# Both attentions: a wide score row's second-half maximum starts from the first half's, and the combining pass on VectorE is dropped

## The chip, the cores and the metric

The kernel runs on one core of a Trainium2 chip. The metric is the device time of one execution in microseconds (us), the median of several runs.

## The reference: two transformer layers with causal attention

The input x is (4, 1024, 128). Four steps follow each other, each added to x behind a layer norm. Only the two attentions matter here; both are causal and have 16 heads.

```python
# first attention (a0 in the kernel), head width 8
scores = jnp.einsum('bhqd,bhkd->bhqk', q, k) * scale
scores = jnp.where(causal, -inf, scores)
attn = jax.nn.softmax(scores, axis=-1)
out = jnp.einsum('bhqk,bhkd->bhqd', attn, v)
...
# second attention (a1), 16 heads over a shared latent of 32 for keys and values
attn = jax.nn.softmax(jnp.where(mask, attn, neg_inf), axis=-1)
```

After each attention comes a mixture of experts (8 experts, two of them chosen, then 16 experts, eight chosen), which the change leaves alone.

## The kernel before: scores are computed twice, once for the maximum of a row and once for the exponential

One function, `attention`, is called for both: as a0 with HG = 4 heads at a time (16 groups) and as a1 with HG = 2 (32 groups). Three kinds of work run interleaved.

**The maxima (S).** For each head the 1024 query rows are cut into eight blocks i = 0 to 7 of 128 rows. Block i sees (i+1)*128 keys. TensorE multiplies queries by keys into one of four PSUM banks `S` of 512 columns (L777). Blocks 4 to 7 are wider than a bank, so they are two units, half 0 with 512 keys and half 1 with the other 128 to 512. I call them 7a and 7b, 6a and 6b and so on, and 3a, 2a, 1a, 0a the narrow ones: 12 units a head, four of them second halves. The order in a head is `BLOCKS`: 7a 7b 3a 6a 6b 2a 5a 5b 1a 4a 4b 0a. For each unit VectorE does three things in a row: a one-column `memset` that carries the wait for TensorE's `unit_ready` (L676), a fused add of the causal mask and maximum over the row (L679, CUSTOM_DVE_ANT_0 in the profile), and the read of its accumulator into `mhalf` ("mh") for half 0 of a wide block or into `mmax` ("m") for all others (the second row of L679, DVE_READ_ACCUMULATOR2_ANT). Behind the last unit of a head, 0a, comes the combining pass: it waits for the last read, and takes the maximum of `mmax` and `mhalf` for the four wide blocks (L686, 128x4). Then TensorE transposes the head's maxima (unit "m", L782), ScalarE copies them negated (L717), and a DMA puts them as one more row into the queries of the next use (`set_row`). Each step that ends on VectorE raises `red_done`; TensorE waits for it before a bank is written again, which is four units later (units m and o count as well).

**The exponentials (T).** For each head nine pieces of 512 columns of transposed scores (L838) go into one of two banks `T`, ScalarE takes the exponential (L736), GpSimd zeroes the triangle on the diagonal (L647). One piece of one head is a slot: 36 slots in a group of a0, 18 in one of a1. TensorE waits before slot n for the exponential of slot n-2.

**The values (V).** Behind every HG-th slot TensorE multiplies a piece's probabilities by the values (L817). ScalarE copies the sums out (L712), TensorE turns them (unit "o", L788), VectorE divides them: a reciprocal (L692), a wait for it, a multiplication (L694).

TensorE's order is written out: slot by slot T, then the S, m or o units that belong to this slot, then V where one is due. The S units of slots are those of a later group: they work one or two groups ahead. In a group of a0 the last head's maxima are turned (m3) in slot 32, directly behind 0a in slot 31 and a V. Slot 33 has 7a 7b, slot 34 has 3a, slot 35 has 6a 6b 2a and a V, and slots 0 to 3 of the next group 5a 5b, 1a, 4a 4b, 0a with a V behind it. Before the first group of each attention stands a start stretch in which only maxima are made: all heads of group 0 and six units of group 1, on a ring of six banks.

Of the kernel before, what the change touches and what calls it, by code (L numbers as in the profile page):

```python
# [10 lines left out]
ALU = mybir.AluOpType  # L11
# [5 lines left out]
BATCH, SEQ = 4, 1024  # L17
TOK = BATCH * SEQ
TILES = TOK // P
ST = 512  # L20
# [430 lines left out]
def attention(k, name, HG, VD, scale, operands, out, work, begin, before_loads, lent=(),  # L451
              PARTS=1, BURST=1, HALVES=2):
    nc, sem = k.nc, k.sem
    NG = BATCH * HEADS // HG
# [9 lines left out]
    LEAD = 4  # L464
    BLOCKS = [b for i in reversed(range(TPB // 2)) for b in (TPB // 2 + i, i)]
    PBUF = 3 * BURST if BURST == 1 else 2 * BURST
    assert NP % BURST == 0 and 2 * NP % PBUF == 0
# [9 lines left out]
    for h in range(HG):  # L477
        blocks = [("S", h, i) for i in BLOCKS]
        chain += blocks[:2] + ([("m", h - 1, 0)] if h else []) + blocks[2:]
    chain.append(("m", HG - 1, 0))  # L480

    def units_from(items):

        return [(kind, h, i, half, ahead, min(n, NSLOT - 1)) for n, (kind, h, i, ahead) in enumerate(items)
                for half in range(HALVES if kind == "o" or kind == "S" and i >= TPB // 2 else 1)]

# [3 lines left out]
    for kind, h, i, half, _, _ in units_from([(*x, 0) for x in chain]):  # L491
        if kind == "S":
            NRED += 3 if i == BLOCKS[-1] and HALVES == 2 else 2
            MAXIMA[h, i, half] = NRED
    lead, own = [(*x, 0) for x in chain[:LEAD]], [(*x, 1) for x in chain[LEAD:]]
    start_units = units_from([(*x, 0) for x in chain] + [(*x, 1) for x in chain[:LEAD]])
    NLEAD = len(units_from(lead))
    NU = len(start_units) - NLEAD
# [3 lines left out]
    assert 2 * (NU + HALVES) % BANKS == 0  # L502
    base_items = own + [(*x, 2) for x in chain[:LEAD]]

    DELAY = HG
    VALUES, CARRIED = ({s: [] for s in range(NSLOT)} for _ in range(2))
    for p in range(NP):
        for part in range(PARTS):  # L510
            s = (p // BURST * BURST + BURST) * HG - 1 + DELAY + part * (HG // PARTS)
            (VALUES[s] if s < NSLOT else CARRIED[s - NSLOT]).append((p, part))
    parts = {}
    for p, piece in enumerate(PIECES):
        off = 0
        for seg in piece:
            for part in range(PARTS):
                c0, c1 = max(off, part * (ST // PARTS)), min(off + seg[2] - seg[1], (part + 1) * (ST // PARTS))
                if c0 < c1:
                    parts.setdefault((p, part), []).append((seg, c0, seg[1] + c0 - off, seg[1] + c1 - off))  # L520
# [3 lines left out]
    COPY_0 = next(s for s in VALUES if (LAST_OF_BANK[0], PARTS - 1) in VALUES[s]) + 1  # L524
    COPY_1 = max(s for s in CARRIED if CARRIED[s]) + 1
    OUT_AT = COPY_1 + 2
    out_item = ("o", 0, 0, -1)
    with_out = lambda items: units_from(items[:OUT_AT] + [out_item] + items[OUT_AT:])

    with ExitStack() as c:  # L530
# [41 lines left out]

        def units_of(g):

            if at(g, NG - 1):
                return [(*x[:5], OUT_AT) for x in units_from([out_item])]
            if at(g, NG - 2):
                return with_out(own)
            return units_from(base_items) if at(g, 0) else with_out(base_items)

        def before(g):

            if at(g, 0):
                last_of = {n % len(start_ring): x for n, x in enumerate(start_units)}
                return [last_of[bank] for bank in main_ring(unit_slot(g))]
            units = units_from(own if at(g, NG - 1) else base_items)
            return [(*x[:4], x[4] - 1, x[5]) for x in units[-BANKS:]]
# [27 lines left out]
        with nc.Block() as block:  # L615
# [37 lines left out]
            def _(dve):  # L653
                def consume(units, base, ring, g):
                    for n, (kind, h, i, half, ahead, _) in enumerate(units):
# [6 lines left out]
                        if kind == "S":  # L662
# [38 lines left out]
                consume(units_from([("o", 0, 0, 0)]), unit_base(END) + HALVES, main_ring(unit_slot(END) + HALVES), END)  # L701

            @block.scalar
            def _(act):
# [21 lines left out]
                def step(g):  # L726
                    units = units_of(g)
                    for p in range(NP):
                        for h in range(HG):
# [16 lines left out]
                            if slot == COPY_0:  # L746
                                copy_out(g, 0)
                            if slot == COPY_1 and not at(g, 0):
# [1674 lines left out]
```

## Time and profile before

| what | value |
|---|---|
| three runs, median (lowest to highest) | 2078.56 us (2075.58 to 2084.6) |
| the profiled execution's own time | 2072.83 us |
| its span | 2071.1 us |
| TensorE matmul busy | 1879.1 us, 91% |
| VectorE busy | 1435.9 us, 69% |
| ScalarE busy | 1193.8 us, 58% |
| GpSimd busy | 622.0 us, 30% |
| first and last start of a T matmul in a0 | 81.6 and 614.7 us |
| the same in a1 | 1038.0 and 1692.9 us |

The two attentions take more than half of the span. The busy time of TensorE counts overlapping matmuls, whose ends are modelled, so 91% is not 91% of its peak.

### The profile page before, as it was taken

The numbers are of one execution on the slowest core, as the hardware profiler recorded it, in microseconds if no ns is written. First come the engines' busy times: TensorE is split into PE (matmuls) and PEld (weight loads), VectorE is DVE, ScalarE is ACT, GpSimd is POOL, SyncE is SP. The second block draws the span as 40 slices with busy tenths as digits, with TensorE's granted clock in tenths as the row PEclk, the third lists the DMA queues.
The fourth block names the chain that finished last, engine by engine and source line by source line (L and its number), as shares of the span: only waits on it lengthen the run. The fifth ranks groups of instructions, "written<-read, shape, count | busy, mean of one in ns | idle before, by whom it ended". The sixth has DMA issues, their size and how long they took to land. (4 is left out here: it accounts for less than half of the span.)

```text
span 2071.1 us, 39995 instructions
## 1 busy us (share of the span) xinstructions
PE 1879.1 (91%) x9924; PEld 1169.6 (56%) x9926; DVE 1435.9 (69%) x6257; ACT 1193.8 (58%) x2252; POOL 622.0 (30%) x955
## 2 busy tenths in 40 slices
PE   5799999999986729994899999999999999899998
PEld 3455555555536527872445555555555558678886
DVE  6788777777826827875766666666666636887776
ACT  5266666666664728981445555555555558555554
POOL 4011111111120774762011111111111110567665
PEclk9799999999995869996989999999999999999999
DMA  6423233433305112224946464655555512546562
GB/s 214 123 35 64 42 61 44 61 48 55 49 8 207 36 56 70 75 76 132 362 112 145 104 139 106 136 111 130 116 126 122 119 35 81 138 93 131 128 121 61
DMA packets 107198, 210.87 MB, mean 102 GB/s; under 512 B 16540, under 2 KB 46378, under 8 KB 105680
## 3 DMA queue, kind: packets, MB, share of 16 engines
q1 hardware_dynamic: 99840, 194.98, 40.8%
q0 software_dynamic: 4992, 8.48, 1.3%
q10 hardware_dynamic: 2256, 6.21, 1.0%
q8 instruction: 37, 0.61, 0.1%
q14 instruction: 73, 0.60, 0.1%
HBM read 163.01 MB, written 47.89 MB: 102 GB/s over the span
## 5 line engine op out<-in xcount | busy, mean ns | idle before, releaser
L679 DVE CUSTOM_DVE_ANT_0 a1ms<-a1S,mask_q 128x128 bf16<-128x128 f32 (+1 forms) x758 | 387.9, 553 | 173.5 <-issue 170.6
L736 ACT ACTIVATE a1work<-a1T 128x512 f32<-128x512 f32 x576 | 330.2, 597 | 297.4 <-PE a1T L838 296.9
L679 DVE CUSTOM_DVE_ANT_0 a0ms<-a0S,mask_q 128x384 bf16<-128x384 f32 (+2 forms) x752 | 379.7, 553 | 97.5 <-issue 90.4
L736 ACT ACTIVATE a0work<-a0T 128x512 f32<-128x512 f32 x576 | 330.0, 597 | 186.6 <-PE a0T L838 175.7
L817 PE MATMUL a1O<-a1work,a1v 128*33 128x512 f32 (+3 forms) x1536 | 304.6, 496 | 0.9 <-POOL a1work L647 0.9
L838 PE MATMUL a0T<-a0qT,a0kT 128*128 128x512 f32 (+3 forms) x768 | 265.3, 392 | 15.9 <-ACT a0work L736 5.1
L838 PE MATMUL a1T<-a1qT,a1kT 97*128 97x512 f32 (+3 forms) x768 | 263.3, 391 | 2.0 <-DMA a1qT<-a1mr 2.0
L838 PEld LDWEIGHTS a1T<-a1qT,a1kT 97*128 97x128 f32 x768 | 131.6, 189 | 202.0 <-ACT a1work L736 144.5
L777 PE MATMUL a0S<-a0kS,a0qS 128*128 128x384 f32 (+2 forms) x752 | 229.9, 362 | 17.2 <-PEq L305 9.1
L1997 POOL TENSOR_TENSOR attn<-attn 128x512 f32<-128x512 f32 x136 | 201.4, 1496 | 105.8 <-DVE attn L1899 104.7
L838 PEld LDWEIGHTS a0T<-a0qT,a0kT 128*128 128x128 f32 x768 | 131.4, 189 | 170.2 <-ACT a0work L736 126.5
L777 PE MATMUL a1S<-a1kS,a1qS 96*128 96x128 f32 (+1 forms) x758 | 219.8, 351 | 2.5 <-DVE a1held L676 1.7
L643 POOL TENSOR_TENSOR a1held<-ident 128x1 f32<-128x1 f32 x160 | 30.9, 193 | 600.6 <-ACT a1work L736 600.6
L1886 DVE TENSOR_TENSOR r1late<-attn,r1late 128x512 fp32r<-128x512 f32 x136 | 120.4, 886 | 70.7 <-ACT r1late L2202 70.3
L643 POOL TENSOR_TENSOR a0held<-ident 128x1 f32<-128x1 f32 x80 | 15.5, 193 | 492.6 <-ACT a0work L736 492.6
L777 PEld LDWEIGHTS a0S<-a0kS,a0qS 128*128 128x128 f32 x752 | 139.7, 195 | 40.6 <-DVE a0held L676 19.2
L2202 ACT CAST r1late<-attn 128x512 fp32r<-128x512 f32 x136 | 84.5, 622 | 133.8 <-POOL attn L1997 127.9
L817 PE MATMUL a0O<-a0work,a0v 128*9 128x512 f32 (+3 forms) x1536 | 150.7, 487 | 0.0
L777 PEld LDWEIGHTS a1S<-a1kS,a1qS 96*128 96x128 f32 x758 | 138.7, 193 | 15.3 <-DVE a1held L676 4.1
L817 PEld LDWEIGHTS a1O<-a1work,a1v 128*33 128x33 f32 x1536 | 64.7, 109 | 108.7 <-issue 81.1
L1365 POOL DMA_INDIRECT scr_pairs<-stage x92 | 104.5, 1136 | 66.5 <-issue 33.4
L1090 DVE TENSOR_TENSOR m_hl<-m_h,m_hh 128x512 fp32r<-128x512 f32 x124 | 85.5, 690 | 32.6 <-ACT m_hh L1524 18.7
(336 smaller groups left out, 3333.2 us busy)
## 6 DMA issues: line engine op xcount, KB each, us to landing
attn<-scr_g SPq DMA_DIRECT2D x32, 1024.0 KB, 9.8
a1qT<-scr_q SPq DMA_DIRECT2D x93, 256.0 KB, 4.1
a1qS<-scr_q SPq DMA_DIRECT2D x90, 256.0 KB, 6.3
a1kT<-scr_k SPq DMA_DIRECT2D x93, 128.0 KB, 4.8
a1kS<-scr_k SPq DMA_DIRECT2D x90, 128.0 KB, 7.0
scr_q<-p_own SPq DMA_DIRECT2D x16, 512.0 KB, 5.1
scr_q<-attn SPq DMA_DIRECT2D x16, 512.0 KB, 7.4
scr_slots<-wp SPq DMA_DIRECT2D x1, 5980.0 KB, 18.2
```

Of the source, the lines that this page charges most:

```text
L643: nc.gpsimd.tensor_tensor(held[:, BANKS + p:BANKS + p + 1], k.ident[:, 0:1], k.ident[:, 0:1], ALU.add).then_inc(masked, 1)
L679: nc.vector.tensor_tensor_reduce(masked_s[spare][:, 0:c1 - c0], buf[:, 0:c1 - c0], k.mask_q[:, SEQ - w + c0:SEQ - w + c1], 1.0, NEVER, ALU ...
L736: nc.scalar.activation(prob_of(g, p)[:, h, :], t_ps[slot % 2][:, :], ACT.Exp, scale=scale)\
L777: last = nc.tensor.matmul(buf[:, c0 - first:c1 - first], qS[gU[1]][0:SROWS, h, i * P:(i + 1) * P], kS[gU[1]][0:SROWS, KI(h), c0:c1], start ...
L817: last = nc.tensor.matmul(o_ps[h * CT:h * CT + VW, q0:q1], vst[g[1]][:, seg[0], KI(h), :], prob_of(g, p)[:, h, off:off + q1 - q0], start=o ...
L838: last = nc.tensor.matmul(t_ps[slot % 2][:, off:off + q1 - q0], kT[g[1]][0:TROWS, KI(h), j * P:(j + 1) * P], qT[g[1]][0:TROWS, h, q0:q1], ...
L1090: tt(hl[n % HBUF][:, :], h[n % 2][:, :], hh[n % HBUF][:, :].bitcast(F32), ALU.subtract).then_inc(hl_ready, 1)
L1365: nc.gpsimd.indirect_dma_start(pair_rows, bass.IndirectOffsetOnAxis(ap=xt[t % XBUF][:, i, D + 1:ROW].bitcast(U32), axis=0), yo[t % XBUF][: ...
L1886: tt(hl[ring(g, e)][:, :], h[two(g, e)], hh[ring(g, e)][:, :].bitcast(F32), ALU.subtract).then_inc(hl_ready, 1)
L1997: nc.gpsimd.tensor_tensor(h[two(g, e)], prod[two(g, e)], gate, ALU.mult).then_inc(h_ready, 1)
L2202: nc.scalar.copy(hh[ring(g, e)][:, :], h[two(g, e)]).then_inc(hh_ready, 1)
```

## The change: the maximum of half 1 is seeded with that of half 0

The fused add-and-maximum takes a start value as its fourth argument from the end: so far the constant NEVER for all units. For half 1 it becomes a column in SBUF, the maximum that half 0 of the same block has left in `mhalf`. So that this column is there, VectorE waits for its own `red_done` ahead of each half 1. The combining pass and its wait go. The rest of the diff writes the options that both calls used (PARTS = 1, BURST = 1, HALVES = 2) into the function, and gives the slot of each unit as a table.

```diff
+class Order:
+    def __init__(self, blocks, mark, units, values, outs):
+        self.blocks, self.mark, self.units, self.values, self.outs = blocks, mark, units, values, outs
+ORDER_0 = Order(((7, 0), (7, 1), (3, 0), (6, 0), (6, 1), (2, 0), (5, 0), (5, 1), (1, 0), (4, 0), (4, 1), (0, 0)),
...
-            NRED += 3 if i == BLOCKS[-1] and HALVES == 2 else 2
+            NRED += 2
...
+                            if half:
+
+                                dve.wait_ge(red_done, lin(gU, NRED, MAXIMA[h, i, 0]))
                             dve.wait_ge(unit_ready, base + (n + 1))
                             nc.vector.memset(held[:, spare:spare + 1], 0.0).then_inc(red_done, 1)
 
                             found = mhalf[par][:, h, i - TPB // 2:i - TPB // 2 + 1] if wide and half == 0 else mmax[par][:, h, i:i + 1]
+                            floor = NEVER
+                            if half:
+                                floor = mhalf[par][:, h, i - TPB // 2:i - TPB // 2 + 1]
                             nc.vector.tensor_tensor_reduce(masked_s[spare][:, 0:c1 - c0], buf[:, 0:c1 - c0],
-                                                           k.mask_q[:, SEQ - w + c0:SEQ - w + c1], 1.0, NEVER,
+                                                           k.mask_q[:, SEQ - w + c0:SEQ - w + c1], 1.0, floor,
                                                            ALU.add, ALU.max, found).then_inc(red_done, 1)
-                            if i == BLOCKS[-1] and HALVES == 2:
-
-                                dve.wait_ge(red_done, lin(gU, NRED, MAXIMA[h, i, half] - 1))
-                                upper = mmax[par][:, h, TPB // 2:TPB]
-                                nc.vector.tensor_tensor(upper, upper, mhalf[par][:, h, :], ALU.max).then_inc(red_done, 1)
...
-                        pe.wait_ge(red_done, lin(gU, NRED, MAXIMA[h, BLOCKS[-1], 0]))
+                        pe.wait_ge(red_done, lin(gU, NRED, HEAD_DONE[h]))
```

In the loops, VectorE's rows for the units 4a, 4b and 0a at the end of a head of a0, with the combining pass behind them, before:

```order
L676 MEMSET a0held 128x1 [waits a0unit]
L679 ISA a0ms,a0mh<-a0S,mask_q 128x512
L679 ISA a0mh 128x1
L675 REGISTER_ALU
L676 MEMSET a0held 128x1 [waits a0unit]
L679 ISA a0ms,a0m<-a0S,mask_q 128x128
L679 ISA a0m 128x1
...
L679 ISA a0m 128x1
L684 ISA
L686 TENSOR_TENSOR a0m<-a0m,a0mh 128x4 [waits a0red]
```

and the same units in the changed kernel:

```order
L681 MEMSET a0held 128x1 [waits a0unit]
L687 ISA a0ms,a0mh<-a0S,mask_q 128x512
L687 ISA a0mh 128x1
L679 REGISTER_ALU
L680 REGISTER_ALU [waits a0red]
L681 MEMSET a0held 128x1 [waits a0unit]
L687 ISA a0ms,a0m<-a0S,mask_q,a0mh 128x128
L687 ISA a0m 128x1
```

Ahead of the second half's memset stands one register instruction more, and it is a register instruction that carries the wait for VectorE's own read; the reduction has a third operand; the combining pass is gone.

For comparison, the same engine's rows for unit o, which both kernels have; the wait for the reciprocal stands there on an instruction of its own too (line numbers of before):

```order
L692 RECIPROCAL a0rec<-a0S 128x16 [waits a0unit]
L693 REGISTER_ALU
L694 ISA [waits a0rec]
L694 TENSOR_TENSOR stage<-a0S,a0rec 128x128
```

On TensorE, ScalarE, GpSimd and SyncE the order is the same in all groups but the first of each attention. There the slot that unit o has in the other groups (6 in a0, 4 in a1) was closed up before and stays empty now, so that the units behind it stand one slot later. TensorE in group 0 of a0, from unit 1.7a on ("a0S 128x512" is a score unit, "a0T" a slot, "8x128" the unit m), before:

```order
MATMUL a0T<-a0qT,a0kT 128x512 [waits a0exp]
MATMUL a0S<-ident,a0m 8x128 [waits a0red]
MATMUL a0T<-a0qT,a0kT 128x512 [waits a0exp]
MATMUL a0S<-a0kS,a0qS 128x512 [waits a0red]
MATMUL a0S<-a0kS,a0qS 128x384 [waits a0red]
```

and in the changed kernel:

```order
MATMUL a0T<-a0qT,a0kT 128x512 [waits a0exp] x2
MATMUL a0S<-ident,a0m 8x128 [waits a0red]
```

## Rows read from the trace of the kernel before

**Rows 1.** The page, part 1: busy us, share of the span, instructions.
```profile
PE 1879.1 (91%) x9924; PEld 1169.6 (56%) x9926; DVE 1435.9 (69%) x6257; ACT 1193.8 (58%) x2252; POOL 622.0 (30%) x955
```

**Rows 2.** Busy time in four stretches; the column before the last two is TensorE's clock.
```profile
54.00:81.00 27.00, 22.16 (x57) 13.95 (x57) 25.27 (x153) 1.06 (x4) 0.00 (x0) 0.63 0.56 184
110.00:590.00 480.00, 464.56 (x2927) 256.89 (x2926) 376.65 (x2158) 313.40 (x607) 80.99 (x187) 1.00 0.33 50
1023.00:1038.00 15.00, 11.35 (x32) 7.28 (x30) 13.75 (x82) 1.80 (x3) 0.00 (x0) 0.64 1.06 400
1060.00:1690.00 630.00, 629.53 (x3258) 321.70 (x3256) 414.06 (x2344) 347.10 (x680) 117.09 (x400) 1.00 0.54 118
```

**Rows 3.** Waits, 110 to 590 us (a0): us in total, times, longest.
```profile
PEld a0T L838 <- ACT a0work L736: 109.9, 226, 0.9
...
PEld a0S L777 <- DVE a0held L676: 12.7, 18, 1.7
...
PEld a0S L782 <- DVE a0m L686: 6.5, 15, 0.7
```

**Rows 4.** Waits, 1060 to 1690 us (a1).
```profile
PEld a1T L838 <- ACT a1work L736: 140.4, 185, 0.8
```

**Rows 5.** Timeline of VectorE, start stretch: start us, duration us, operation.
```profile
59.80 0.08 DVE L679 DVE_READ_ACCUMULATOR2_ANT a0mh<- 128x1 f32 x1
59.81 0.28 DVE L679 CUSTOM_DVE_ANT_0 a0ms<-a0O,mask_q 128x128 bf16<-128x128 f32 x1
59.83 0.06 DVE L676 MEMSET a0held<- 128x1 f32 x1
...
60.24 0.08 DVE L679 DVE_READ_ACCUMULATOR2_ANT a0m<- 128x1 f32 x1
60.36 0.16 DVE L686 TENSOR_TENSOR a0m<-a0m,a0mh 128x4 f32<-128x4 f32 x1
...
60.51 0.69 DVE L679 CUSTOM_DVE_ANT_0 a0ms<-a0S,mask_q 128x512 bf16<-128x512 f32 x1
```

**Rows 6.** The same, a1: unit o, with its wait for the reciprocal.
```profile
1315.41 0.20 DVE L692 RECIPROCAL a1rec<-a1S 128x8 f32<-128x8 f32 x1
1315.75 0.42 DVE L694 TENSOR_TENSOR attn<-a1S,a1rec 128x256 f32 x1
```

**Rows 7.** TensorE behind the start stretch of a0.
```profile
89.53 0.80 PE L838 MATMUL a0T<-a0qT,a0kT 128*128 128x512 f32 x1 [4.58 <-DMA a0qT<-a0mr]
```

**Rows 8.** Groups by line and shape: busy us, mean ns, idle before.
```profile
L686 DVE TENSOR_TENSOR a0m<-a0m,a0mh 128x4 f32<-128x4 f32 x64 | 20.0, 312 | 2.2
...
L212 DVE TENSOR_SCALAR stage<-x,mean,rstd 128x128 f32<-128x128 f32 x64 | 17.4, 365 | 0.5 <-PEq L181 0.5
```

**Rows 9.** One group of a0, slots 31 to 36: VectorE, with one row of GpSimd.
```profile
316.26 0.64 POOL L647 TENSOR_SCALAR_AFFINE_SELECT a0work<-a0work 128x512 f32<-128x512 f32 x1
...
316.28 0.08 DVE L679 DVE_READ_ACCUMULATOR2_ANT a0m<- 128x1 f32 x1
316.40 0.51 DVE L686 TENSOR_TENSOR a0m<-a0m,a0mh 128x4 f32<-128x4 f32 x1
...
322.28 0.08 DVE L679 DVE_READ_ACCUMULATOR2_ANT a0m<- 128x1 f32 x1
```

**Rows 10.** The same slots: TensorE (PE) and its weight loads (PEld).
```profile
316.38 0.49 PE L838 MATMUL a0T<-a0qT,a0kT 128*128 128x512 f32 x1
...
316.96 0.08 PEld L782 LDWEIGHTS a0S<-ident,a0m 128*8 128x8 f32 x1 [0.40 <-DVE a0m L686]
...
317.05 0.50 PE L838 MATMUL a0T<-a0qT,a0kT 128*128 128x512 f32 x1
...
317.38 0.63 PE L777 MATMUL a0S<-a0kS,a0qS 128*128 128x512 f32 x2
...
319.19 0.19 PEld L777 LDWEIGHTS a0S<-a0kS,a0qS 128*128 128x128 f32 x1 [0.41 <-DVE a0held L676]
...
322.71 0.22 PE L777 MATMUL a0S<-a0kS,a0qS 128*128 128x128 f32 x1
```

More of the change, by code:

```diff
@@ L463, in attention @@
     NLOAD = operands.NLOAD
[L464 to L467, printed above, removed]
+    LEAD, PBUF = 6, 3
+    assert 2 * NP % PBUF == 0
     DIAGONALS = [[(off, seg) for off, seg in zip((0, p[0][2] - p[0][1]), p) if seg[1] == seg[0] * P] for p in PIECES]
@@ L477, in attention @@
     for h in range(HG):
[L478 to L486, printed above, removed]
+        blocks = [("S", h, *x) for x in order.blocks]
+        chain += blocks[:order.mark] + ([("m", h - 1, 0, 0)] if h else []) + blocks[order.mark:]
+    chain.append(("m", HG - 1, 0, 0))
     MAXIMA, NRED = {}, 0
-    for kind, h, i, half, _, _ in units_from([(*x, 0) for x in chain]):
+    for kind, h, i, half in chain:
         if kind == "S":
-            NRED += 3 if i == BLOCKS[-1] and HALVES == 2 else 2
+            NRED += 2
             MAXIMA[h, i, half] = NRED
[L495 to L498, printed above, removed]
+    HEAD_DONE = [max(n for (head, _, _), n in MAXIMA.items() if head == h) for h in range(HG)]
+    start_units = [(*x, 0, 0) for x in chain] + [(*x, 1, 0) for x in chain[:LEAD]]
+    NLEAD, NU = LEAD, len(chain)
     START_MAXIMA = NRED + MAXIMA[start_units[-1][1:4]]
@@ L501, in attention @@
     BANKS = 2 * HALVES
-    assert 2 * (NU + HALVES) % BANKS == 0
-    base_items = own + [(*x, 2) for x in chain[:LEAD]]
-    DELAY = HG
+    assert 2 * (NU + HALVES) % BANKS == 0 and len(order.units) == NU
+    ahead_units = [(*x, a, slot) for (x, a), slot in zip([(x, 1) for x in chain[LEAD:]] + [(x, 2) for x in chain[:LEAD]], order.units)]
+    out_units = [("o", 0, 0, half, -1, slot) for half, slot in enumerate(order.outs)]
+    last_outs = [("o", 0, 0, half, 0, 0) for half in range(HALVES)]
     VALUES, CARRIED = ({s: [] for s in range(NSLOT)} for _ in range(2))
[L509 to L514, printed above, removed]
+    for p, s in enumerate(order.values):
+        (VALUES[s] if s < NSLOT else CARRIED[s - NSLOT]).append(p)
+    segments = []
+    for piece in PIECES:
         off = 0
+        segments.append([])
         for seg in piece:
[L517 to L520, printed above, removed]
+            segments[-1].append((seg, off, seg[1], seg[2]))
             off += seg[2] - seg[1]
     LAST_OF_BANK = [max(p for p, piece in enumerate(PIECES) if any(s[1] // ST == b for s in piece)) for b in range(2)]
[L524 to L528, printed above, removed]
+    COPY_AT = [order.values[p] + 1 for p in LAST_OF_BANK]
     with ExitStack() as c:
@@ L585, in before @@
                 return [last_of[bank] for bank in main_ring(unit_slot(g))]
-            units = units_from(own if at(g, NG - 1) else base_items)
-            return [(*x[:4], x[4] - 1, x[5]) for x in units[-BANKS:]]
+            return [(*x[:4], x[4] - 1, x[5]) for x in units_of(after(g, -1))[-BANKS:]]
         def beside(units, slot):
@@ L745, in step @@
                                     copy_max(unit_base(g), main_ring(unit_slot(g)), n, gm, hm)
[L746 to L749 removed]
+                            for b in range(SEQ // ST):
+                                if slot == COPY_AT[b]:
+                                    copy_out(g, b)
+                                if slot == COPY_AT[b] - NSLOT and not at(g, 0):
+                                    copy_out(after(g, -1), b)
                 main_steps(act, step)
[L752 removed]
+                for b in range(SEQ // ST):
+                    if COPY_AT[b] >= NSLOT:
+                        copy_out(END, b)
             @block.tensor
@@ L809, in values @@
                             nc.tensor.matmul(o_ps[:, b * ST:(b + 1) * ST], zero[:, 0:P], zero, start=True, stop=True)
-                    if part == 0 and p < SEQ // ST and not at(g, 0):
+                    if p < SEQ // ST and not at(g, 0):
                         pe.wait_ge(o_copied, lin(g, 2, p - 1))
-                    for x in parts[p, part]:
+                    for x in segments[p]:
                         seg, off, q0, q1 = x
@@ L818, in values @@
                                                     prob_of(g, p)[:, h, off:off + q1 - q0],
-                                                    start=opens[bank] == (p, part, *x), stop=closes[bank] == (p, part, *x))
-                    if part == PARTS - 1:
-                        last.then_inc(pv_done, 1)
+                                                    start=opens[bank] == (p, x), stop=closes[bank] == (p, x))
+                    last.then_inc(pv_done, 1)
                 def step(g):
```

54 lines of the change are left out of this document (29 added, 25 removed), and 4 rows, old and new, of the table ORDER_0.

## The prediction, written before the changed kernel had run

> **What bounds the kernel now.** The page comes first: TensorE is busy for 91% of the span and VectorE for 69% [rows 1]. So a shorter VectorE is worth only what TensorE waits for it, and the change touches nothing outside the two attentions. The table by stretch splits these into four. In the steady stretch of a0 (480 us) TensorE is busy for 464.56 and VectorE for 376.65; in that of a1 (630 us) TensorE shows 629.53 and VectorE 414.06. The two start stretches are the other way round: VectorE is busy for 25.27 of 27 us and 13.75 of 15 us, at a TensorE clock of 0.63 and 0.64 [rows 2]. The start stretches are VectorE's.
>
> The list of waits says who holds TensorE in the steady stretches. In a0 it is ScalarE with 109.9 us ahead of T; VectorE follows with 12.7 us ahead of S (a bank not yet reduced) and 6.5 us ahead of the unit m [rows 3]. In a1 the longest is ScalarE again, 140.4 us [rows 4], and VectorE does not occur in that list. The waits of a weight load partly lie under matmuls that still stream, so they are upper bounds: VectorE's together could give back at most 19 us.
>
> **The wait that is added.** Per head there are four second halves. Now a second half follows the first at once: the read of mh starts at 59.80 and the memset of 4b at 59.83, 0.03 later [rows 5]. Afterwards this memset may start only when the read has ended and been seen. Two rows bound the cost. The combining pass waits for a read in just this way, with the wait on itself: read at 60.24, pass at 60.36, 0.12 against 0.03, so 0.09 us more [rows 5]. In unit o the wait stands on a register instruction of its own, as it will here: the reciprocal ends at 1315.41 + 0.20 = 1315.61 and the product starts at 1315.75, 0.14 behind the end [rows 6]. With the read's 0.08 that is 0.22 against 0.03, so 0.19 us. In the changed order the wait is of the second kind. I take 0.17 us a second half, near the upper row.
>
> The new operand, one value per partition from SBUF, isn't in the trace for this operation. The nearest row is a tensor_scalar with two such operands, 365 ns for 128 columns; the reduction of 128 columns without one takes 0.28 us [rows 5, 8]. Half of the difference is 0.04 us for one operand, and part of it may be another cause. I take nothing, and keep up to 0.1 for the range (the full difference and some contention). A cost of w below covers both.
>
> **The combining pass that goes.** In the start stretch a read starts at 60.24 and the next reduction at 60.51 instead of 0.01 behind the read (59.80 to 59.81 is what an unhindered step shows): 0.26 us a head [rows 5]. In the steady stretch of a0 the pass takes 312 ns in the mean against 0.16 us in the start stretch [rows 5, 8]. One of them shows why: it starts at 316.40, takes 0.51 and ends at 316.91, and GpSimd's masking runs from 316.26 to 316.90 [rows 9]. The Trainium skill (SBUF — State Buffer, Who interferes with whom) says that a VectorE instruction with two SBUF inputs is blocked by a GpSimd one that reads SBUF; the row agrees. What stays afterwards is a reduction that reads PSUM, the mask in SBUF, and the new scalar. Whether that scalar makes it a second SBUF input, the page doesn't say; it is a rival below.
>
> Net per head on VectorE: 4 x 0.17 - 0.26 = +0.42 us where GpSimd is silent, and 4 x 0.17 - 0.26 - 0.15 = +0.27 us in a0. So in spite of 128 instructions less VectorE gets a little more to do.
>
> **The sum, place by place.**
>
> Start stretches: VectorE is the bound, so all of it counts. A start stretch makes group 0's heads and six units of group 1, two of them second halves. a0: 18 x 0.17 - 4 x 0.26 = +2.0 us. a1: 10 x 0.17 - 2 x 0.26 = +1.2 us. The first group of a0 then waits 4.58 us for the DMA of its fourth row of maxima [rows 7]. If that transfer is late because of other traffic rather than its own start, it hides the 2.0. I count it, since the row is issued behind the fourth head's m.
>
> Steady stretch of a0, one group of four heads: there are two places where TensorE waits for VectorE, and one that comes near. (1) m3: TensorE starts T at 316.38 and m3 at 316.96. Behind an unhindered T the next unit starts 0.33 later (317.05 to 317.38), so m3 could stand at 316.72: it costs 0.24 [rows 10]. It waits for the pass that ends at 316.91. Ahead of it lie, back to back, 5a 5b 1a 4a 4b 0a with two second halves: the last read, which ends at 316.36 now, will end at 316.36 + 0.34 = 316.70 [rows 9]. The wait falls by 0.2. (2) 2a in slot 35 waits for 7b's bank; its weights are loaded at 319.19 and had waited 0.41 [rows 10]. 7b is a second half: -0.2 from the earlier 7a, + 0.17, so V behind it starts 0.03 earlier. Nothing of (1) is left over. (3) VectorE then runs through 3a 6a 6b 2a 5a 5b with two more second halves: 5b's read, done at 322.36 now, is done at 322.36 - 0.03 + 0.34 = 322.67. TensorE's 0a, at 322.71 now, needs that bank [rows 9, 10]. It would start at 322.68 and needs some 0.05 behind the read (m3's weights stand 0.05 behind the pass): +0.04. Behind it VectorE waits for TensorE again, and the account starts afresh. Sum +0.01 us a group, 16 groups: +0.2 us.
>
> Steady stretch of a1: VectorE is busy for 66% [rows 2] and is waited for nowhere [rows 4]. A head has 10 us there and gets 0.42 more: 0.
>
> First groups: their units behind the empty slot stand one slot later, in two of 48 groups. The slot is empty in both kernels in all other groups; 0.
>
> Sum 2.0 + 1.2 + 0.2 = +3.4 us. On the profiled execution's 2072.8 that is 2076.2; but that execution is 5.7 below the median of the three runs, which I go by: 2078.6 + 3.4 = **2082 us**. Half a per cent, 10.4 us, is about what a measurement of this kernel can tell from no change.
>
> **The rivals.**
>
> Small gain (w = 0.09 or less). The wait would cost what the combining pass's does: start stretches 28 x 0.09 - 6 x 0.26 = +1.0; in a0 the whole 0.24 of m3 goes, and 0.15 of it survives 7b: -2.4. Sum -1.4 us, 2077. With w = 0 it is -1.6 and 16 x -0.24 = -3.8: -5.4 us, 2073. The Trainium skill (VectorE: DVE Perf Modes, The DRAIN you can't avoid, and Rules for kernel authors) would have it so: a semaphore between VectorE operations costs nothing extra, and it is the count of operations that should fall. Against it stand 0.12 behind a read with a wait and 0.01 without one [rows 5]. If TensorE's wait ahead of 2a went as well (0.41 on the weights [rows 10]), there would be 16 x 0.65 = 10.4 us at the most, the edge of a visible gain. Chance of a time below 2079: 0.2.
>
> Slower by a visible amount (w = 0.25 to 0.3). The scalar makes the reduction dearer, or makes it a second SBUF input that waits for GpSimd, which is busy for 81 of 480 us in a0 [rows 2]. At w = 0.25 the start stretches cost 28 x 0.25 - 1.6 = +5.4. In a0 m3's wait falls by 0.04 only, 7b comes 0.2 later and V with it, and 5b's read is done at 322.36 + 0.2 + 0.5 = 323.06, while 0a would start at 322.91: 0.2 more. That is 0.4 a group, 16 x 0.4 = +6.4. Sum +12 us, 2090. At 0.3 it is 0.05 + 0.3 + 0.3 = 0.65 a group: 10.4 + 6.8 = +17 us, 2096. From w = 0.17 on each 0.1 us more costs some 10 us; that is the point from which it decides. Chance 0.22.
>
> Less arrives: the start of a0 is hidden behind the DMA's 4.58 us [rows 7]. Then +1.4 us, 2080. It is in the likeliest case's range (0.58 together, 2079 to 2087).
>
> **How the numbers follow.** Likeliest: 2082. Range 2068 (the small gain at its most, 10.4 off) to 2096 (w = 0.3). Faster by over 0.5% needs every wait of a0 for VectorE to go: 0.1. Slower by over 0.5% needs w of 0.24 or more: 0.19. Within: 0.71.
>
> **What would show it.** In the start stretch the memset of a second half should stand 0.03 + 0.17 = 0.2 behind the start of the read ahead of it, and each stretch be 2.0 and 1.2 us longer. The reduction of a half 1 with 128 columns should keep its 0.28 us; if it is longer, or long when GpSimd masks, the slower rival holds. No L686 or its like. In a0 the wait of m for VectorE (6.5 us) should fall to some 2, that of S for VectorE (12.7) should rise. a1's steady stretch should be as long as now. The prediction is wrong if TensorE in a0 waits for 0a's bank by more than 0.1 a group, or if VectorE's new wait costs nothing.

## The result, and the profile after

The changed kernel takes **2104.75 us** in the median of four runs (2104.08 to 2105.65); the kernel before, run beside it, takes 2077.07 us (2073.8 to 2084.6). The ratio is 1.0128, with a 95% interval of 1.01 to 1.0157. It is slower by 1.3%, where 2082 us and no visible change were forecast; the time lies outside the range too. The profiled execution has a span of 2102.6 us, against 2071.1.

The page's part 1, after, answers to [rows 1]:

```profile
PE 1897.9 (90%) x9924; PEld 1173.6 (56%) x9926; DVE 1487.0 (71%) x6129; ACT 1197.2 (57%) x2252; POOL 624.5 (30%) x955
```

TensorE has not one instruction more, and is busy for 18.8 us longer; that is already a hint at its clock. The stretches that answer to [rows 2], after (the start of a0, its steady stretch, the same two of a1):

```profile
55.09:86.30 31.21, 26.07 (x58) 15.17 (x57) 27.84 (x150) 1.07 (x4) 0.00 (x0) 0.50 0.48 153
115.00:615.00 500.00, 477.83 (x2902) 258.99 (x2901) 393.60 (x2101) 311.06 (x602) 81.27 (x187) 0.98 0.33 48
1052.42:1069.58 17.16, 13.04 (x31) 7.77 (x30) 14.60 (x77) 1.77 (x3) 0.00 (x0) 0.54 1.06 376
1092.00:1722.00 630.00, 629.52 (x3258) 324.02 (x3256) 442.92 (x2284) 347.15 (x681) 117.66 (x401) 1.00 0.54 118
```

The steady stretch of a0 had a clock of 1.00 and has 0.98. That of a1 has not changed. From the first reduction to the first T, and from there to the last T, the two traces give:

| stretch | before | after | longer by | forecast |
|---|---|---|---|---|
| a0, start | 27.16 | 31.21 | 4.05 | 2.0 |
| a0, first to last T | 533.14 | 557.64 | 24.5 | 0.2 |
| a1, start | 14.96 | 17.16 | 2.2 | 1.2 |
| a1, first to last T | 654.93 | 655.23 | 0.3 | 0 |

Four fifths of the difference of 31.5 us stand in one row, and it is the row that had been forecast as nothing. The waits in a0 after the change (115 to 615 us), which answer to [rows 3]:

```profile
PEld a0T L842 <- ACT a0work L739: 105.9, 221, 0.9
...
DVE a0held L681 <- DVE a0mh L687: 26.2, 170, 0.2
PEld a0S L783 <- DVE a0held L681: 19.4, 52, 0.8
PEld a0S L783 <- DVE a0mh L687: 14.8, 12, 2.8
DVE a0held L681 <- issue: 11.1, 5, 2.4
PE a0S L783 <- DVE a0mh L687: 10.8, 5, 2.4
...
PEld a0S L788 <- DVE a0m L687: 4.5, 15, 0.3
```

The wait of m for VectorE fell, from 6.5 to 4.5 us. But there are five waits of TensorE for VectorE of over 2 us each, and in the same number five idle times of VectorE with the releaser "issue". Five is neither the number of second halves nor of groups: it is the number of times that a0's loop jumps back (six passes over two groups each). One of the five, first VectorE (start, duration, operation), after:

```profile
225.28 0.08 DVE L687 DVE_READ_ACCUMULATOR2_ANT a0mh<- 128x1 f32 x1
225.52 0.06 DVE L681 MEMSET a0held<- 128x1 f32 x1 [0.15 <-DVE a0mh L687]
225.56 0.62 DVE L687 CUSTOM_DVE_ANT_0 a0ms<-a0S,mask_q,a0mh 128x384 bf16<-128x384 f32 x1
...
226.14 0.06 DVE L681 MEMSET a0held<- 128x1 f32 x1
226.59 0.08 DVE L687 DVE_READ_ACCUMULATOR2_ANT a0m<- 128x1 f32 x1
229.10 0.06 DVE L681 MEMSET a0held<- 128x1 f32 x1 [2.42 <-issue]
```

The same place in the kernel before:

```profile
219.61 0.06 DVE L676 MEMSET a0held<- 128x1 f32 x1
220.06 0.08 DVE L679 DVE_READ_ACCUMULATOR2_ANT a0m<- 128x1 f32 x1
221.55 0.06 DVE L676 MEMSET a0held<- 128x1 f32 x1 [1.41 <-PE a0S L777]
```

And TensorE there, after:

```profile
227.14 0.40 PE L783 MATMUL a0S<-a0kS,a0qS 128*128 128x512 f32 x1
229.90 0.33 PE L783 MATMUL a0S<-a0kS,a0qS 128*128 128x128 f32 x1 [2.37 <-DVE a0mh L687]
230.06 0.45 PE L842 MATMUL a0T<-a0qT,a0kT 128*128 128x512 f32 x1
230.59 0.33 PE L783 MATMUL a0S<-a0kS,a0qS 128*128 128x128 f32 x1
230.85 1.70 PE L822 MATMUL a0O<-a0work,a0v 128*9 128x512 f32 x8
232.47 0.79 PE L842 MATMUL a0T<-a0qT,a0kT 128*128 128x512 f32 x1
...
236.20 1.05 PE L822 MATMUL a0O<-a0work,a0v 128*9 128x512 f32 x8
```

Behind the standstill of 2.37 us the eight matmuls of V take 1.70 instead of 1.05 us, and a T 0.79 instead of 0.50. The stretches around it (TensorE's clock is the third column from the end), after:

```profile
219.00:227.40 8.40, 8.05 (x47) 4.04 (x47) 6.14 (x35) 5.12 (x11) 0.78 (x2) 1.00 0.04 6
...
230.00:232.00 2.00, 1.93 (x11) 0.50 (x11) 1.84 (x13) 0.60 (x1) 0.77 (x2) 0.78 0.00 0
232.00:234.00 2.00, 2.00 (x8) 1.24 (x5) 0.54 (x7) 0.62 (x2) 0.01 (x1) 0.50 0.11 25
234.00:236.00 2.00, 2.00 (x13) 1.65 (x12) 1.84 (x9) 1.56 (x3) 0.00 (x0) 0.87 0.54 92
236.00:244.00 8.00, 7.87 (x50) 4.30 (x52) 6.29 (x37) 5.33 (x10) 1.37 (x3) 1.00 0.56 75
```

```profile
222.36 0.33 PE L777 MATMUL a0S<-a0kS,a0qS 128*128 128x128 f32 x1 [1.02 <-DVE a0held L676]
```

and by stretch:

```profile
222.30:224.00 1.70, 1.64 (x12) 0.66 (x12) 1.70 (x16) 0.60 (x1) 0.32 (x2) 1.00 0.00 0
```

What happens between is seen in the trace's register and branch instructions, which the profile doesn't count as busy. VectorE's, with the end of the last read ahead and the next memset, in us:

```
                    jump (COMPARE_BRANCH)   last read ends   next instruction behind the jump   memset
before   L597       218.56                  220.15           221.41 (2.85 behind the jump)      221.55
after    L599       225.93                  226.67           228.95 (3.02 behind the jump)      229.10
```

This jump costs VectorE 2.8 to 3.1 us in which no new instruction comes; that is the range of all ten in a0, five before and five after. Before, it is carried out 1.59 us ahead of the end of the last reduction: the stream of instructions had run ahead while three reductions were queued. After, the stream stands in front of 6b's wait until 6a's maximum has been read. Only the reductions of 6b and 2a are then left to cover the jump, and it lies 0.75 us ahead of the last end. (The last units of a group are head 0's 6a, 6b and 2a; then comes the jump, then 5a.)

It is not the price of every jump. The loop of a1 jumps back 13 times in each of the two traces, and there VectorE's next register instruction comes 0.27 to 0.32 us behind the jump; on TensorE, ScalarE, GpSimd and SyncE it comes 0.16 to 0.33 us behind theirs, in a0 as in a1. A pass of a0's loop has 422 recorded instructions on VectorE before and 438 after, one of a1's 222 and 230, and a0's on TensorE 616. Why the one loop pays ten times the other's price was not tested: no run changed the length of a pass alone.

The Trainium skill (Runtime: NRT & Kernel Launch, Instruction fetch mechanics) says that a taken branch breaks the sequential prefetch, and forces a fetch of the target's page before execution goes on when the target is not in the current window of two pages; it gives an engine's instruction memory as 512 instructions, and TensorE's as 2048. It gives no duration. The trace agrees in so far as the long pass of VectorE alone has such a stall, with 2.85 and 3.02 us; that the window is the reason isn't shown.

The wait itself, and the operand. VectorE's timeline in the start stretch, after, which answers to [rows 5]:

```profile
61.26 0.08 DVE L687 DVE_READ_ACCUMULATOR2_ANT a0mh<- 128x1 f32 x1
61.46 0.06 DVE L681 MEMSET a0held<- 128x1 f32 x1
```

and its groups by line and shape in a0 (115 to 615 us; busy us, mean ns), after:

```profile
L687 DVE CUSTOM_DVE_ANT_0 a0ms<-a0S,mask_q 128x512 bf16<-128x512 f32 x284 | 193.8, 686 | 58.9 <-issue 58.5
L687 DVE CUSTOM_DVE_ANT_0 a0ms<-a0S,mask_q,a0mh 128x512 bf16<-128x512 f32 x56 | 42.0, 750 | 0.3
...
L687 DVE CUSTOM_DVE_ANT_0 a0ms<-a0S,mask_q,a0mh 128x128 bf16<-128x128 f32 x57 | 19.9, 350 | 0.4
...
L687 DVE CUSTOM_DVE_ANT_0 a0ms<-a0S,mask_q 128x128 bf16<-128x128 f32 x57 | 16.3, 286 | 0.0
```

From read to memset it is 0.20 us in the start and 0.24 in the groups (225.28 to 225.52), instead of 0.03. The reduction with the scalar takes 64 ns more at 128 and at 512 columns. It also starts 0.04 behind its memset (225.52 to 225.56) where one without a wait starts 0.03 ahead. That belongs to the wait and not to the operand: the one unit with a wait and no operand, in before_one_wait below, does the same (217.44 to 217.48), and in pointer_only the reductions with the operand and no wait start 0.03 ahead. So in the groups the wait moves the reduction by 0.27 us and the operand lengthens it by 0.06. Together a second half costs 0.34 us, twice the 0.17 that the forecast went by.

### The profile page after: what moved, and what is told of

Its sections match the earlier page's. It is cut to its first block and busy times, and to the rows that moved or that the text cites. A ratio compares the mean times of both kernels' runs of the same rounds, so it can differ in the third digit from the quotient of the medians.

```text
span 2102.6 us, 40249 instructions
## 1 busy us (share of the span) xinstructions
PE 1897.9 (90%) x9924; PEld 1173.6 (56%) x9926; DVE 1487.0 (71%) x6129; ACT 1197.2 (57%) x2252; POOL 624.5 (30%) x955
## 5 line engine op out<-in xcount | busy, mean ns | idle before, releaser
L687 DVE CUSTOM_DVE_ANT_0 a1ms<-a1S,mask_q 128x512 bf16<-128x512 f32 (+1 forms) x506 | 292.3, 586 | 114.6 <-issue 113.7
L687 DVE CUSTOM_DVE_ANT_0 a0ms<-a0S,mask_q 128x512 bf16<-128x512 f32 (+2 forms) x502 | 286.3, 586 | 73.8 <-issue 64.9
L783 PE MATMUL a0S<-a0kS,a0qS 128*128 128x384 f32 (+2 forms) x752 | 239.0, 373 | 27.5 <-DVE a0mh L687 10.8
L645 POOL TENSOR_TENSOR a0held<-ident 128x1 f32<-128x1 f32 x80 | 15.6, 195 | 521.9 <-ACT a0work L739 521.9
L687 DVE CUSTOM_DVE_ANT_0 a1ms<-a1S,mask_q,a1mh 128x512 bf16<-128x512 f32 x252 | 138.8, 551 | 1.0
L687 DVE CUSTOM_DVE_ANT_0 a0ms<-a0S,mask_q,a0mh 128x256 bf16<-128x256 f32 (+1 forms) x250 | 137.6, 550 | 2.0
```

What stands on the lines that cost most here:

```text
L645: nc.gpsimd.tensor_tensor(held[:, BANKS + p:BANKS + p + 1], k.ident[:, 0:1], k.ident[:, 0:1], ALU.add).then_inc(masked, 1)
L783: last = nc.tensor.matmul(buf[:, c0 - first:c1 - first], qS[gU[1]][0:SROWS, h, i * P:(i + 1) * P], kS[gU[1]][0:SROWS, KI(h), c0:c1], start ...
```

## The experiments

Theory L: VectorE's jump, uncovered by the new waits, makes most of it, and TensorE's clock falls behind the standstill. Its rivals: D, the dearer reduction makes it; S, the plain sum of all waits makes it, with no special place. Each kernel was timed in five rounds against the kernel before. "Slots" is the time from the first to the last T in the profiled execution, "gaps" the mean standstill of TensorE at the five jumps of a0, and "falls" says behind how many of the five TensorE's clock fell to 1.2 GHz. Each fall took 1.7 us of full speed, as above (one in wait_only 3.3).

| kernel | median us | ratio to before (95%) | a0 start, slots | gaps | falls |
|---|---|---|---|---|---|
| wait_only | 2097.81 | 1.0105 (1.0083 to 1.0128) | 30.34, 555.73 | 2.27 | 4 |
| pointer_only | 2072.99 | 0.9988 (0.9972 to 1.0005) | 27.13, 536.51 | 1.04 | 0 |
| neither | 2068.42 | 0.9962 (0.995 to 0.9974) | 26.17, 532.29 | 1.15 | 0 |
| apart | 2076.07 | 1.0002 (0.9989 to 1.0014) | 27.14, 536.99 | 1.32 | 2 |
| before_one_wait | 2085.4 | 1.0053 (1.0036 to 1.007) | 27.16, 541.88 | 2.23 | 2 |
| after_one_free | 2091.4 | 1.0075 (1.006 to 1.009) | 31.24, 547.00 | 0.96 | 1 |
| after_written_out | 2078.1 | 1.0011 (0.9997 to 1.0024) | 31.22, 530.86 | none | |
| before_written_out | 2064.2 | 0.9948 (0.9935 to 0.9961) | 26.51, 523.10 | none | |
| wait_written_out | 2073.27 | 0.9981 (0.9965 to 0.9998) | 30.34, 524.15 | none | |
| apart_written_out | 2067.33 | 0.9958 (0.9945 to 0.9971) | 27.14, 531.21 | none | |
| before_all_written_out | 2066.98 | 0.9956 (0.9941 to 0.9972) | 27.16, 523.80 | none | |
| after_all_written_out | 2073.11 | 0.9988 (0.9976 to 1) | 31.24, 527.37 | none | |

"None" means no standstill that comes back with every second group; one to three single ones of 0.6 to 1.6 us occur there at changing places. The clock fell behind one of these, 1.61 us long, in wait_written_out. The kernel before has gaps of 1.02 and no fall by the same measure, the changed kernel 2.17 and five.

### The parts of the change, one by one

wait_only, against the changed kernel:

```diff
-                            if half:
-                                floor = mhalf[par][:, h, i - TPB // 2:i - TPB // 2 + 1]
```

> The changed kernel with the constant as start value again; the wait ahead of each half 1 stays, and nothing joins the two halves, so the first half of a wide row doesn't count in the maximum. Theory L (the wait is the main part: it holds VectorE's instruction stream, so that the loop's jump at the end of every second group of a0 is taken late and its some 2.4 us stand bare; TensorE's clock falls behind that gap): the read-to-memset distance stays 0.24 us, the gaps of TensorE of 2 us in a0 stay, and the time is 2090 to 2098. Rival D (the scalar operand is the main part: 0.13 us more for each second half loads VectorE): the time falls to 2077 to 2085 and the gaps shrink to the 1 us of before.

pointer_only:

```diff
-                            if half:
-                                dve.wait_ge(red_done, lin(gU, NRED, MAXIMA[h, i, 0]))
...
-                                floor = mhalf[par][:, h, i - TPB // 2:i - TPB // 2 + 1]
+                                floor = k.eps[:, 0:1]
```

> The changed kernel without the wait; the start value of half 1 is a constant column in SBUF, so the reduction has its third operand but depends on nothing, and the first half of a wide row doesn't count in the maximum. Theory L: no bare jump, no fall of the clock; the start stretches net about nothing (28 x 0.1 - 1.6 us), 2073 to 2080, like before. Rival D: 2088 to 2098.

neither has both edits, wait and operand left out, and no combining pass; like the two above it, it leaves the first half's maximum out of the result:

> The changed kernel without the wait and with the constant as start value: the combining pass is gone and nothing takes its place, so the first half of a wide row doesn't count in the maximum. This is what the removal alone is worth. Both theories: start stretches -1.6 us, a0 some -0.2 to -0.5 us in each of 16 groups: 2068 to 2074. If it is no faster than before, VectorE isn't waited for in a0 at all and the losses must come from elsewhere.

apart moves the units and keeps everything else, in both attentions (the whole result is computed):

```diff
-ORDER_0 = Order(((7, 0), (7, 1), (3, 0), (6, 0), (6, 1), (2, 0), (5, 0), (5, 1), (1, 0), (4, 0), (4, 1), (0, 0)),
+ORDER_0 = Order(((7, 0), (6, 0), (7, 1), (3, 0), (6, 1), (2, 0), (5, 0), (4, 0), (5, 1), (1, 0), (4, 1), (0, 0)),
```

> The changed kernel, whole computation, with the units of a head in the order 7a 6a 7b 3a 6b 2a 5a 4a 5b 1a 4b 0a: one unit stands between a first half and its second, so the wait finds its read done while VectorE still has work queued, and two units stand between the last first half and the loop's jump. Theory L: the jump is covered again, the clock stays up, the wait costs little; what stays is the scalar's 0.06 to 0.13: 2074 to 2082. Rival D: the scalar's cost is all there, 2095 to 2104.

The wait alone brings the five long gaps and nearly all of the time; the operand alone brings no long gap. D falls as an account of the whole. Against the kernel with neither the operand costs 4.6 us (2072.99 to 2068.42), but that isn't shown to be its own price: of the 4.2 us between their slots (536.51 and 532.29) 3.3 are longer waits of TensorE for the DMA that loads the keys (6.6 against 3.3 us), and such waits differ from kernel to kernel. The start stretch of a0 splits cleanly: the wait costs 30.34 - 26.17 = 4.17 us for 18 second halves, 0.23 each; the operand 0.96, 0.05 each; the combining pass 27.16 - 26.17 = 0.99, where 1.04 had been forecast. With the halves apart the condition of the wait is met before the stream gets to it: the memset of the second half stands 0.03 us behind the read again. The whole 1.3% is gone, though the gaps are 0.3 us longer than in the kernel before and the clock fell behind two of them.

### One wait, and one wait less

before_one_wait is the kernel before with one line more:

```diff
+                            if half and (h, i, g[1]) == (0, 6, 1) and not isinstance(g[0], int):
+                                dve.wait_ge(red_done, lin(gU, NRED, MAXIMA[h, i, 0]))
```

> The kernel before with one wait more, in front of one unit only: the second half of block 6 of head 0, in the second group of the loop's body, which is the last second half ahead of the loop's jump back (six times in the first attention, as many in the second). Theory L (that wait holds VectorE's instruction stream, so that the jump, some 2.9 us from jump to next instruction, is no longer covered by queued reductions, TensorE stands still for over 2 us and then runs some us at half its clock): 5 gaps of TensorE of 2 us or more in the first attention, 1.2 us dearer each and 1 to 2.5 us more for the clock, 11 to 19 us in all, so 2086 to 2094 beside a kernel before of 2075. Theory S (the time comes from the sum of all the waits, 0.34 us per second half, which use up the spare time of VectorE over a group): one wait per two groups costs 6 x 0.17 = 1 us, so 2075 to 2077.

after_one_free is the changed kernel with that one unit exempt:

```diff
-                            if half:
+                            joined = half and ((h, i, g[1]) != (0, 6, 1) or isinstance(g[0], int))
+                            if joined:
                                 dve.wait_ge(red_done, lin(gU, NRED, MAXIMA[h, i, 0]))
...
-                            if half:
+                            if joined:
                                 floor = mhalf[par][:, h, i - TPB // 2:i - TPB // 2 + 1]
```

> The changed kernel, with the wait and the scalar operand left out in that one unit (second half of block 6 of head 0, second group of the loop's body), all others kept. It leaves the first half's maximum of those rows out of the result. Theory L: the jump is covered again by the reductions queued behind the wait of the unit ahead; the five long gaps are back at 1.2 us or less, no half clock, and what stays is the start (some 6 us for both attentions) and 1 us for a group without a jump: 2080 to 2088, against 2104 for the changed kernel. Theory S: 12 of 768 waits less, 2101 to 2104.

These two are the sharpest. One wait per two groups costs the kernel before 9.6 us (2085.4 to 2075.8), where the sum of waits gives 1: S falls as an account of the jump's part. (The edit reaches 6 units of a0 and 14 of a1, whose loop has 14 passes, not 6 and 6 as the expectation has it; a1's slots are no longer for it, 654.48 against 654.93 us. In after_one_free, too, it is 20 of 512 second halves, not 12 of 768.) L's lower end, 2086, was just missed. The timelines of VectorE and TensorE in before_one_wait:

```profile
218.45 0.08 DVE L681 DVE_READ_ACCUMULATOR2_ANT a0m<- 128x1 f32 x1
221.07 0.06 DVE L678 MEMSET a0held<- 128x1 f32 x1 [2.54 <-issue]
...
221.88 0.33 PE L779 MATMUL a0S<-a0kS,a0qS 128*128 128x128 f32 x1 [2.42 <-DVE a0held L678]
...
222.49 1.90 PE L819 MATMUL a0O<-a0work,a0v 128*9 128x512 f32 x8
```

and a stretch of it:

```profile
224.00:226.00 2.00, 2.00 (x8) 1.41 (x5) 0.41 (x2) 0.77 (x2) 0.00 (x0) 0.52 0.14 29
```

Here the picture of the changed kernel has been made with one wait, clock and all. The jump is carried out 0.69 us ahead of the last end, the next instruction comes 3.08 behind it. All five gaps are long (2.12 to 2.42 us), but the clock fell behind two of them only, this one and the third. Behind the second, of 2.33 us, and the third:

```profile
292.00:300.00 8.00, 8.00 (x52) 4.88 (x55) 6.61 (x36) 5.53 (x11) 0.78 (x2) 1.00 0.41 62
361.00:369.00 8.00, 7.96 (x41) 4.93 (x42) 5.31 (x30) 4.11 (x8) 0.78 (x2) 0.79 0.37 63
```

So the longer gap is what one wait makes every time, and the fall of the clock follows it only sometimes. The gaps add 11.14 - 5.12 = 6.0 us and the two falls 2 x 1.7 = 3.4, together 9.4 of the 9.6. The other way round, one wait less of the 32 of two groups, with its operand, takes 13.4 us off the changed kernel (2104.75 to 2091.4). The jump stands 1.59 us ahead of the last end again. The steady stretch (110 to 590 us) has its clock back but for one fall, behind a gap of 0.92:

```profile
110.00:590.00 480.00, 464.26 (x2858) 252.89 (x2856) 387.50 (x2073) 304.90 (x588) 78.86 (x182) 1.00 0.31 50
```

and its list of waits has the five at the jumps with 4.8 us in sum, 1.1 at the longest:

```profile
PE a0S L784 <- DVE a0mh L688: 4.8, 5, 1.1
```

But 2091.4 is 3 us above L's range of 2080 to 2088: L alone had given the groups 1 us, and they cost more. In this profiled execution a0's slots are 547.00 - 533.14 = 13.9 us longer than in the kernel before, with gaps no longer than there (0.96 and 1.02) and the first group's wait for its DMA the same within 0.24 us (4.34 and 4.58). By medians the whole difference is 2091.4 - 2075.8 = 15.6, and 9.4 without the 6.2 of the two starts. So the waits and operands apart from the jump cost the groups of a0 some 9 to 14 us.

### The loop written out

In after_written_out and before_written_out VectorE alone has no loop:

```diff
-                main_steps(dve, lambda g: consume(units_of(g), unit_base(g), main_ring(unit_slot(g)), g))
+                for u in range(NG // 2):
+                    for par in range(2):
+                        g = (u, par)
+                        consume(units_of(g), unit_base(g), main_ring(unit_slot(g)), g)
```

> The changed kernel with VectorE's loop of the attentions written out (14 more copies of the two groups' instructions in place of the loop, same instructions and waits, no jump on VectorE; the other engines keep their loops). Theory L: no gap of TensorE over 1.3 us in the steady part of the first attention and its clock at 1.00 there; 2080 to 2090. Theory S: waits and reductions are the same, 2101 to 2105. If long straight code itself has to be fetched at a price, the time could be higher than the kernel's with the loop; then gaps would show at other places than every second group.

> The kernel before with VectorE's loop written out in the same way. Its five gaps of 0.94 to 1.25 us beside the jump, against none elsewhere, are what the jump still costs in it: by theory L they go, 5 x 1.0 = 5 us, 2069 to 2072 beside 2075. By theory S, no change: 2074 to 2076.

wait_written_out and apart_written_out have the same edit on wait_only and on apart:

> The changed kernel with the waits but without the scalar operand (the first half's maximum does not enter the second's, and there is no combining pass), VectorE's loop written out. It splits what is left of the change once the jump is gone (2078 against 2064 us for the two kernels with the loop written out, 14 us). Theory 1, the waits make it: 4 us in the start of the first attention, 2 in that of the second and the rest in the groups: 2072 to 2076. Theory 2, the dearer reduction (64 ns longer, 66 ns later) makes most of it: 2066 to 2070.

> The changed kernel with each second half behind another reduction in both orders (7 first half, 6 first half, 7 second, 3, 6 second, 2, 5 first, 4 first, 5 second, 1, 4 second, 0) and VectorE's loop written out; the whole result is computed. With the loop it ran at 1.000 of the kernel before. The jump's share in it should be as in the kernel before (five gaps of 1.2 to 1.5 us): 2062 to 2068 by theory L, 2074 to 2077 if the gain of writing out depended on the old order.

before_all_written_out and after_all_written_out write it out on every engine (main_steps, `for u in range(1, NG // 2 - 1)` in place of the loop):

> The kernel before with the loop of the attentions written out on all five engines, not on VectorE alone (2064 us). If only VectorE's jump is exposed, because the other engines' streams run ahead of their work: 2062 to 2066, as with VectorE alone. If TensorE's or ScalarE's jump costs anything too: under 2060.

> The changed kernel with the loop written out on all five engines. By the theory that the jump that counts is VectorE's: 2076 to 2080, as with VectorE's alone (2078). If the part left of the change came from jumps of other engines: 2066 to 2072.

Writing the loop out takes away more than the jump, though the expectation speaks of the same instructions and waits. VectorE's register instructions (ALU_OP) fall from 1630 to 198 in the kernel before (1942 to 198 in the changed one), and the wait for VectorE's own read no longer stands on a register instruction but on the memset itself:

```profile
226.33 0.08 DVE L687 DVE_READ_ACCUMULATOR2_ANT a0mh<- 128x1 f32 x1
226.45 0.48 DVE L687 CUSTOM_DVE_ANT_0 a0ms<-a0S,mask_q,a0mh 128x256 bf16<-128x256 f32 x1
226.48 0.06 DVE L681 MEMSET a0held<- 128x1 f32 x1
```

The reduction stands 0.12 us behind the read instead of 0.28 (0.01 without a wait). So these kernels show what is left without the jump and with the wait at less than half its price, and no run separates the two.

In this form the changed kernel is at 1.0011, and the kernel before at 0.9948: 11.6 us less, more than the 5 of its own five gaps that had been expected (2064.2, not 2069 to 2072). 10.0 of them are in a0's slots, 533.14 - 523.10; the gaps are 5.12 of that. Another 3.8 may come from the first group's wait for its DMA, 0.76 us here and 4.58 in the kernel before, ahead of any jump. The rest wasn't traced further. a1's loop gives nothing: its slots take 654.9 us with it and 654.5 without, and its jump takes only 0.3 us. The waits in after_written_out (110 to 590 us) have kept only the short ones:

```profile
PEld a0S L786 <- DVE a0held L681: 7.9, 27, 0.6
PEld a0S L791 <- DVE a0m L687: 2.7, 15, 0.2
...
PE a0S L786 <- DVE a0held L681: 0.8, 3, 0.3
```

The others' jumps take 0.16 to 0.33 us and cost nothing that can be told: with all five engines written out the kernel before takes 2066.98 (2061.86 to 2075.56). The changed kernel's 2073.11 is 5 us below the expected 2076 to 2080, in runs that spread from 2069.37 to 2079.12; whether another engine's jump costs the changed kernel some us stays open.

By these medians the change costs 2078.1 - 2064.2 = 13.9 us without the jump. The stretches give 31.22 - 26.51 = 4.7 in the start of a0, 17.11 - 14.96 = 2.15 in that of a1, and 530.86 - 523.10 = 7.8 in a0's slots. But 4.4 of the 7.8 are longer waits for DMAs (the first group's 3.42 against 0.76, the keys' 2.5 against 0.8), and the pair with all engines written out, where the two kernels differ by 0.3 in these waits, is only 527.37 - 523.80 = 3.6 us apart in the slots and 6.1 by medians (2073.11 to 2066.98). So with the cheaper wait a0's slots lose some 3.5 us (an estimate from these differences). How this splits between wait and operand is open: the medians give the waits 9.1 (the saved pass in it) and the operand 4.8, the slots 1.0 (524.15) and 6.7, and the profiled execution of wait_written_out was 5 us faster than that kernel's median, in runs that spread by 16 us. The median of wait_written_out lies in the range of theory 1, its profiled execution (2068.03) in that of theory 2: neither is shown.

## Why the prediction was wrong

**The failed step** is the one that counted a group of a0 in slots 31 to 36 and multiplied by 16: "Sum +0.01 us a group, 16 groups: +0.2 us". The groups are not alike. Every second one ends in VectorE's jump back, and there the wait does something that its own length doesn't show: it keeps the stream of instructions from running ahead. By after_one_free it is 13.4 us of 28 in the medians and 557.64 - 547.00 = 10.6 in the slots. Counted piece by piece in the trace of the changed kernel it is 5.7 us of longer gaps (10.83 against 5.12 in sum) and 5 x 1.7 = 8.5 us of lost clock, 14.2. The written-out pair gives (2104.75 - 2078.1) - (2075.8 - 2064.2) = 15.0, with the cheaper wait in it. So it is 11 to 15 us. The prediction looked only for units queued behind the waiting one; the jump was queued there too. The five gaps of 0.94 to 1.25 us of the kernel before stood in its waits for VectorE, and the prediction went by their sum.

**The size of the wait**, w, was 0.17 with bounds of 0.09 and 0.19 for the wait and up to 0.1 for the operand. It is 0.34 in the groups (0.27 and 0.06) and 0.28 in the start by the stretches (0.23 and 0.05). The memset is where the row of unit o had put it, 0.21 us later (0.24 instead of 0.03); what the sum left out is that the reduction then starts behind its memset instead of ahead of it (0.07), and the operand (0.06), for which it took nothing. This is the second cause: the starts cost 6.25 instead of 3.2 us, and the groups of a0 9 to 14 us instead of 0.2 (after_one_free). The visibly slower rival had this mechanism, with 0.4 a group at w = 0.25 and 0.65 at 0.3, and 2090 to 2096 in all. Carried on to 0.34 at the same slope it gives 0.85 a group, 13.6 us, an estimate from the rival's own figures. after_one_free, at 2091.4, is the changed kernel with little more than this part; the rival's chance of 0.22 was too small, and it lacked the jump.

**The combining pass** was rightly sized. The small-gain rival had reckoned -5.4 us for no wait at all; neither, beside 2074.94, brought -6.5. The gain exists and is paid for more than twice by what takes its place.

**The steady stretch of a1** was right: 654.93 to 655.23, with no wait of TensorE for VectorE, though VectorE waits 34.5 us for itself there. Its loop jumps back too, at 0.3 us a jump.

**The DMA rival** came true in part: the wait for the fourth row of maxima fell from 4.58 to 3.03 us [rows 7], so 1.55 of the 4.05 us that the start lost may have been hidden. In the other kernels this wait lies between 0.76 and 4.34 with no order that follows the start, so no more can be said.

**GpSimd** did not slow the reduction with the scalar: 350 and 750 ns in a0's groups, and 0.35 and 0.75 us in the start stretch, where GpSimd is silent. Over both attentions 33 of the 128 reductions of 512 columns with the scalar ran while GpSimd masked; they took 750 ns in the mean, and so did the other 95.

**The parts of a0's 24.5 us.** after_one_free splits them into 10.6 and 13.9. Its five gaps are 6.0 us shorter in sum than the changed kernel's and it has four falls of the clock less, 6.8 us; that is 12.9, not 10.6. Of the 2.3 us between, 1.3 are its longer wait for the first group's DMA (4.34 against 3.03); the rest stays open.

## What to carry to other kernels

A wait that an engine makes on its own last result costs more than its 0.3 us where a dear jump follows. Look for the jump in the trace and read how long it takes there (3 us in a0's loop, 0.3 in a1's). Ask how much queued work covers it, and let one more unit stand between a result and the wait for it (the order "apart" gave the whole loss back). Before the last link of a chain is rearranged, try writing out the loop of the engine that is waited for; here that alone made 2064.2 us of 2075.8. The best whole form of this change, apart_written_out with 2067.33, is not faster (0.9958 beside 0.9948, with intervals that overlap).

## What was not expected of the hardware

- VectorE's jump back in a0: 2.75 to 3.10 us from the jump to the next instruction, in 20 jumps of four kernels' traces (before, after, before_one_wait, after_one_free), covered only by what is queued. In before_one_wait 0.9 us less cover turned a gap of 1.02 into one of 2.42 us. In a1's shorter loop the same jump takes 0.27 to 0.32 us.
- A wait for VectorE's own last read moves the next reduction by 0.27 us where it stands on a register instruction, and by 0.12 where it stands on the memset (after_written_out).
- TensorE's clock in the full stream of a0 fell to 1.2 GHz behind 11 of the 15 standstills of 2.1 to 2.4 us at jumps (after, wait_only, before_one_wait), and behind 3 of the 25 of 0.9 to 1.5 us (before, pointer_only, neither, apart, after_one_free). A fall cost 1.7 us of full speed, one of them 3.3. So the length of a standstill alone doesn't say whether the clock falls: behind 2.33 us it stayed at 2.4 GHz, behind 0.92 it fell once.
- One scalar per partition from SBUF in the masked reduction: 63 to 64 ns longer at all four widths (350, 483, 617, 750 against 286, 420, 553, 686 ns). That is not the 0.04 us that half the difference of two other rows had suggested.
